# Node sums of a four-layer graph network by segmented running sums along the edges, stored to DRAM and gathered at each node's last edge, in place of one-hot products added into SBUF

## What is computed

```
x = ln(x + L0(x, edge_attr, src, dst))   # segment_sum(x[src] + edge_attr@We + b) -> MLP 64-128-64
x = ln(x + L1(x, src, dst))              # sum, sum of squares, max, min of x[src]; scalers by degree;
                                         # 768x64 product; batch norm; relu
x = ln(x + L2(x, src, dst))              # mean of x[src] @ w_l.T + x @ w_r.T + b
x = ln(x + L3(x, W, weight, src, dst, etype))  # segment_sum((x @ W[etype])[src] * weight)
```

## Time and profile before

| | |
|---|---|
| median of three runs | 16,712.28 us |
| the profiled execution, first to last instruction (span; the page gives no other time of it) | 22,127.4 us |
| POOL busy | 12,342.5 us (56%) |
| PE busy (matmul) | 8,912.5 us (40%) |
| DVE busy | 8,596.8 us (39%) |
| ACT busy | 1,783.1 us (8%) |
| mean traffic | 33 GB/s |

### The profile page before, as it was taken

The page is one execution under the profiler, slowest core; times in us unless marked ns, Lnnn a source line. Parts: engine busy times, 40 slices in busy tenths (PEclk is TensorE's granted clock), DMA queues, the critical chain, the costliest instruction groups (busy, mean ns, idle before and its releaser), DMA issues. The chain is left out here.

```text
span 22127.4 us, 244411 instructions
## 1 busy us (share of the span) xinstructions
PE 8912.5 (40%) x46268; PEld 7719.6 (35%) x46268; DVE 8596.8 (39%) x26793; ACT 1783.1 (8%) x5619; POOL 12342.5 (56%) x12921
## 2 busy tenths in 40 slices
PE   3444444445555555555553333333334333333333
PEld 3334333334544444444442222222223222222222
DVE  4333333333455555555553333333334333333333
ACT  0000000000222222222220000000001000000000
POOL 5555555555555555555545555655564555555555
PEclk6666666666677777777775555555555555555555
DMA  2222222221111111111111111111112111111111
GB/s 62 43 40 41 40 40 40 39 40 39 40 38 37 37 37 38 38 38 37 38 44 26 22 23 22 23 22 22 23 23 69 23 23 23 23 23 23 23 23 33
DMA packets 1780784, 739.62 MB, mean 33 GB/s; under 512 B 1449213, under 2 KB 1566897, under 8 KB 1777102
## 3 DMA queue, kind: packets, MB, share of 16 engines
q0 software_dynamic: 412800, 423.23, 10.0%
q1 hardware_dynamic: 1367936, 315.87, 7.1%
HBM read 669.74 MB, written 68.37 MB: 33 GB/s over the span
## 5 line engine op out<-in xcount | busy, mean ns | idle before, releaser
L1188 DVE TENSOR_TENSOR acc<-acc,ps_o 64x128 f32 (+2 forms) x12500 | 4373.1, 350 | 12651.9 <-remote 6628.2
L638 POOL DMA_INDIRECT work<-x_table,index x6250 | 5904.8, 945 | 4822.7 <-DMA window<-window_d 2837.1
L898 PE MATMUL ps_o<-work 128*64 128x128 f32 x12500 | 3079.6, 427 | 6978.2 <-issue 2381.0
L898 PEld LDWEIGHTS ps_o<-work 128*64 128x64 f32 x12500 | 2436.2, 223 | 7613.9 <-DVE acc L1188 4474.7
L638 POOL DMA_INDIRECT work<-x_in,index x3125 | 3001.3, 960 | 2400.2 <-DMA window<-window_d 1515.1
L638 POOL DMA_INDIRECT work<-xw_table,index x3125 | 2955.0, 946 | 2102.9 <-DMA window<-window_d 1106.8
L892 PE MATMUL ps_o<-work 128*66 128x128 f32 x6250 | 1692.7, 365 | 3127.2 <-DVE acc L1188 1371.0
L1164 DVE TENSOR_SCALAR work<-iota,meta 128x128 f32<-128x128 f32 x9375 | 2851.2, 304 | 69.8 <-issue 67.1
L895 PE MATMUL ps_o<-work 128*128 128x128 f32 x6250 | 1560.4, 339 | 2698.4 <-ACT work L707 1788.5
L892 PEld LDWEIGHTS ps_o<-work 128*66 128x66 f32 x6250 | 1083.7, 194 | 3308.3 <-DVE acc L1188 1887.2
L895 PEld LDWEIGHTS ps_o<-work 128*128 128x128 f32 x6250 | 1196.2, 238 | 2860.9 <-DVE acc L1188 1933.5
(11 more groups left out here) (201 smaller groups left out, 3977.0 us busy)
## 6 DMA issues: line engine op xcount, KB each, us to landing
work<-edge_attr SPq DMA_DIRECT2D x625, 160.0 KB
restart<-restart_d SPq DMA_DIRECT2D x625, 160.0 KB
work<-x_table,index POOLq DMA_INDIRECT x6250
work<-x_in,index POOLq DMA_INDIRECT x3125
work<-xw_table,index POOLq DMA_INDIRECT x3125
meta<-meta_d SPq DMA_DIRECT2D x2500, 7.5 KB
window<-window_d SPq DMA_DIRECT2D x2500, 0.0 KB
index<-src_e SPq DMA_DIRECT2D x1875, 2.5 KB
```

Source lines behind the costliest of these rows:

```text
L638: pool.indirect_dma_start(out=xs[:, q, k, col:col + D], out_offset=None, in_=table, in_offset=bass.IndirectOffsetOnAxis(ap=index[:, q, k:k ...
L898: ins = pe.matmul(sums[k][0:D, 0, :], xs[:, q, k, 0:D], s, start=True, stop=True)
L1188: dve.tensor_tensor(a, a, sums[k][0:n_rows, 0:halves, :], ALU.add).then_inc(L.added, 1)
```

## The change

The gathers of the edge phase stay as they are, 3,125 a layer in slots of five. Everything behind them is another method. PE turns the slot's rows so that features lie on partitions and 640 edges along the columns (`turn_in`). DVE runs one scan over the 640 columns (`scan`), whose factor is 0 at the first edge of a node and 1 elsewhere, so that the running sum starts anew with each node; it goes on from the last column of the slot before. In layer 1 there are two scans, one for sums and squares and one for maxima. PE turns the result back into rows (`turn_back`), ACT copies them from PSUM (`take_rows`) and stores all of them, for every edge, to a DRAM array `dump` (`dump_rows`), a DMA on ACT's own queue. A stored slot has 128 partitions of 2,560 bytes in layers 0 and 1 (two such stores in layer 1) and of 1,280 bytes in layers 2 and 3.

In the node phase POOL gathers, for each tile of 128 nodes, the row of each node's last edge from `dump`: 98 indirect DMAs a layer, 196 in layer 1 (two arrays). The row numbers come from a histogram of `dst` that PE and DVE make beside the first 62 turns of layer 0 (`one_hots`, `count_edges`: ten bf16 products a slot). A node phase has 14 groups of 7 tiles, written out without a loop. The dense products stay in f32; the bf16 parts are gone.

The core of the diff (`L.n` is the layer, `L.streams` 2 in layer 1 and 1 elsewhere):

```diff
-                def load_slot(turn, q, _, L=L):
-                    sp.wait_ge(L.added, block_no(turn, q, SUB))
-                    s = step_no(turn, q)
-                    rows = xw_rows_d if L.n == 3 else src_e
-                    sp.dma_start(index[:, q, :], rows[:, bass.ds(s * SUB, SUB)]).then_inc(meta_loaded[q], 16)
-                    sp.dma_start(meta[:, q, :], meta_v[:, bass.ds(s, 1), :].rearrange("p s f -> p (s f)")) \
-                        .then_inc(meta_loaded[q], 16)
-                    sp.dma_start(window[:, q, :], window_d.unsqueeze(0)[:, bass.ds(s * SUB, SUB)]) \
-                        .then_inc(meta_loaded[q], 16)
...
+                def load_slot(turn, q, L=L):
+                    if first(turn):
+                        return
+                    s = slot_no(turn, q)
                     if L.n == 3:
-                        sp.dma_start(weight[:, q, :], weight_e[:, bass.ds(s * SUB, SUB)]).then_inc(aux_loaded[q], 16)
+                        sp.wait_ge(L.prep, s + 1)
+                    else:
+                        sp.wait_ge(gathered[q], gathers_landed(L, turn - 1))
+                    sp.sem_inc(sp_past, 1)
+                    load_index(L, turn, q)
+                    for j in range(L.streams):
+                        sp.wait_ge(L.scan[j], s + 1)
+                    sp.sem_inc(sp_past, 1)
+                    load_flags(L, turn, q)
...
-                def scatter(turn, q, t, L=L):
-                    if t == 0:
-                        pool.wait_ge(L.rows_out if L.n else L.rows_set, step_no(turn, q) + (1, 3, 2, 2)[L.n])
-                        pool.sem_inc(pool_past, 1)
-                    pool.indirect_dma_start(
-                        out=agg[L.n], out_offset=bass.IndirectOffsetOnAxis(ap=node_of[:, q, t:t + 1], axis=0),
-                        in_=L.rows[:, q, t, 0:D], in_offset=None, bounds_check=N - 1, oob_is_err=False,
-                    ).then_inc(scattered[q], 16)
...
+                def gather(turn, q, L=L, table=table, col=col):
+                    pool.wait_ge(index_loaded[q], index_there(L, turn))
+                    for j in range(L.streams):
+                        pool.wait_ge(L.turned[j], slot_no(turn, q) + 1)
+                    pool.sem_inc(pool_past, 1)
+                    for k in range(SUB):
+                        pool.indirect_dma_start(
+                            out=xs[:, q, k, col:col + D], out_offset=None, in_=table,
+                            in_offset=bass.IndirectOffsetOnAxis(ap=index[:, q, k:k + 1], axis=0),
+                        ).then_inc(gathered[q], 16)
...
+                        for taken in (L.tp if L.n == 1 else [L.taken]):
+                            pool.wait_ge(taken, g - RING + 1)
+                    for t in range(GRP):
+                        for j in range(L.streams):
+                            pool.indirect_dma_start(
+                                out=L.agg[:, g % RING, t, j * L.span:(j + 1) * L.span], out_offset=None, in_=dump[L.n][j],
+                                in_offset=bass.IndirectOffsetOnAxis(ap=node_row[:, g * GRP + t:g * GRP + t + 1], axis=0),
+                            ).then_inc(agg_loaded[g % RING], 16)
...
+                        act.wait_ge(dumped[q], dumps_landed(L, turn - 1))
+                    elif L.n == 0:
+                        act.wait_ge(flags_stored, 32)
+                    for j in range(L.streams):
+                        act.wait_ge(L.back[j], SLOTS + s + 1)
+                        act.activation(L.rows[j][:, q], back_buffer(L, q, j)[:, 0:SUB * L.span], ACT.Copy) \
+                            .then_inc(L.rowed[j], 1)
...
+                def dump_rows(turn, q, L=L, dump_v=dump_v, chunk=chunk):
+                    s = slot_no(turn, q)
+                    for j in range(L.streams):
+                        act.wait_ge(L.rowed[j], SLOTS + s + 1)
+                        act.sem_inc(act_past, 1)
+                        act.dma_start(dump_v[j][:, bass.ds(s * chunk, chunk)], L.rows[j][:, q]).then_inc(dumped[q], 16)
...
-                    s = onehot[:, q, k, :]
-                    elif L.n == 1:
-                        pe.matmul(sums[k][:, 0, :], xs[:, q, k, D:3 * D], s, start=True, stop=True)
-                        ins = pe.matmul(sums[k][:, 1, :], turned[:, q, k, :], s, start=True, stop=True)
-                    else:
-                        ins = pe.matmul(sums[k][0:D, 0, :], xs[:, q, k, 0:D], s, start=True, stop=True)
-                    ins.then_inc(L.summed, 1)
...
+                def turn_back(turn, q, L=L):
+                    s = slot_no(turn, q)
+                    for j in range(L.streams):
+                        pe.wait_ge(L.scan[j], SLOTS + s + 1)
+                        pe.wait_ge(L.rowed[j], SLOTS + s if L.n < 2 or q == 0 else SLOTS - 1 + s)
+                        pe.sem_inc(pe_past, 1)
+                        to = back_buffer(L, q, j)
+                        for k in range(SUB):
+                            ins = pe.transpose(to[:, k * L.span:(k + 1) * L.span], scanned[j][0:L.span, q, k * P:(k + 1) * P],
+                                               ident[0:L.span, 0:L.span])
+                        ins.then_inc(L.back[j], 1)
...
-                def add(turn, q, k, L=L, n_rows=n_rows, halves=halves, first_rank=first_rank):
-                    if k == 0:
-                        _, first_rank["of"] = nc.values_load_multi_w_load_instructions(
-                            window[0:1, q, :], engines=[mybir.EngineType.DVE], min_val=0, max_val=N - 1,
-                            skip_runtime_bounds_check_because="a rank is less than the number of nodes")
-                    n = block_no(turn, q, k)
-                    dve.wait_ge(L.summed, CREDIT + n + 1)
-                    dve.wait_ge(L.added, CREDIT + n)
-                    a = acc[0:n_rows, 0:halves, bass.ds(first_rank["of"][k], P)]
-                    dve.tensor_tensor(a, a, sums[k][0:n_rows, 0:halves, :], ALU.add).then_inc(L.added, 1)
...
+                    for j in range(L.streams):
+                        dve.wait_ge(L.turned[j], SLOTS + s + 1)
+                        dve.wait_ge(L.back[j], s + 1)
+                        dve.wait_ge(L.scan[j], SLOTS + s)
+                        op0, op1 = (ALU.mult, ALU.add) if j == 0 else (ALU.add, ALU.max)
+                        dve.tensor_tensor_scan(scanned[j][0:L.span, q, :], flags[0:L.span, q, j, :],
+                                               turned_buffer(L, q, j)[0:L.span, 0:SE],
+                                               scanned[j][0:L.span, (q - 1) % SLOTS, SE - 1:SE], op0, op1) \
...
```

More of the change, by code:

```diff
@@ L56 @@
+LAST = N - (P - 1) * NT
+GRP = 7
+GROUPS = NT // GRP
+GW = GRP * D
+RING = 3
+assert GROUPS * GRP == NT and 0 < LAST < NT
+HB = 10
+HIST_TURNS = 62
+HIST_COLS = NT * D // 2
+HIST_LAST = BLOCKS - HIST_TURNS * SLOTS * HB
+NODE_TURN = 70
 AVG_D_LOG = 2.833
 EPS = 1e-5
-RESTART = -1e30
-F_REL, F_END, F_DST = 0, 5, 10
-FIELDS = 15
-XS_COLS = 192
-L0_ROWS = 66
-DEG, DST = 64, 65
-def pipeline(eng, turns, stages, parts=1, start=0):
-    for q in range(SLOTS):
-        for part in range(parts):
+RESTART = 2.0 ** 100
@@ L436, in flat @@
-        def flat(tiles):
-            return tiles.rearrange("p t f -> p (t f)")
+            L.streams, L.span = STREAMS[n], SPAN[n]
+            L.width = L.streams * L.span
+            chunk = SUB * L.span
+            L.rows = [rows_all[:, :, j * chunk:(j + 1) * chunk] for j in range(L.streams)]
+            L.turned = [ls(f"turned{j}") for j in range(L.streams)]
+            L.scan = [ls(f"scan{j}") for j in range(L.streams)]
+            L.back = [ls(f"back{j}") for j in range(L.streams)]
@@ L1449 @@
         "weight_e": turned(inputs["edge_weight"]),
+        "dst_e": turned(inputs["dst"]),
         "dst_n": arr("dst", EP, EW),
```

1722 lines of the change are left out of this document (767 added, 955 removed).

## The result

The changed kernel takes 17,282.72 us (median of four runs, 17,248.87 to 17,293.49) against 16,714.6 us for the kernel before (median of four, one more than in the table of the time before); the ratio is 1.0335 [1.0321, 1.035]. It is 3.4% slower where 0.4% faster was predicted, and lies above the range. The profiled execution took 17,273.66 us, so this time profile and timed runs agree.

A forecast was written before the change was run, and what follows sets the result against it. The prediction took POOL issuing 12,500 gathers back to back as the bound: 15,600 us, plus 20 for the head, 980 for node phases and 45 of rest, 16,645, given as 16,650 us; range 16,350 to 16,930.

The forecast's parts named there:

- All lie beside the gathers.: Edge phases: DVE, PE and ACT each need under 6.24 us a slot, so POOL's 15,600 us of gathers stays.
- 22 ns at most: Layer 0's gathers: the most the trace shows they could shorten when DVE's one-hots and their two-port mode go.
- The allowance of 10 us for DVE's pauses: Layer 0: row numbers after turn 62 and 6,272-column operations at turn 70 cost 10 us, inside the 45 kept.
- The head: Start of the kernel: POOL issues 25 gathers before PE's first turn, so it costs 20 us, not 52.8.
- The estimate of 51 us for the first turn of PE: Head: 27 us for flags, 5.6 for a store to land and 18 for constants come before PE's first turn.
- The node phases: Phases after each layer's edge phase: 165, 370, 300 and 145 us, 980 in sum against 1,014.4 before.
- The clock decides, to the slow side: Rival: PE gets 1.2 GHz in the node phases of layers 1 and 2, giving 16,780 us; chance 0.18.
- Its threshold: The clock rival decides above a node-phase sum of 1,093 us, 33 us over the median.
- The stores: Rival: stores lengthen gathers by 80 ns, 250 us in layer 1 alone: 16,900 us, or 17,650 in all layers; chance 0.12.
- the quick gathers: Rival: timed gathers are quicker than profiled ones and DVE set the time before: 12,850 us, halfway 14,750; chance 0.08.
- the lost interference: Rival: gathers shorten to 938 ns, 22 ns in layer 0 and 7 elsewhere, 134 us, giving 16,515; chance 0.08.
- the first paragraph's reading of the earlier trace: Profile before: POOL's 5,459.0 us of waits for `window` loads are mostly of the profile's making and left out.

The follow-up runs named there:

- c1: Changed kernel, layer-1 stores cut to 8 of 640 columns, layer 1's node phase gathering from layer 0's array, ACT's DMA issues kept: 17,266.54 us.
- c2: Changed kernel with one more ACT operation of 320 columns in each layer-1 slot, written to unused memory: 17,143.76 us.
- e2: Changed kernel with one more ACT operation per layer-1 slot, and ACT's copies and stores there one slot later: 16,925.34 us.
- b1: Changed kernel with ACT's layer-1 copies and stores one slot later, one-hots' iota in PSUM, PE's first credits before the constants: 16,757.58 us.
- c3: Changed kernel with two more DVE additions a slot, layer 2 with both operands in SBUF, layer 3 with one in PSUM: 17,550.95 us.
- c4: b1 with SyncE's constants loaded in parts behind turns 2 to 8, its wait for row numbers three turns later: 16,667.17 us.
- groups a and d: Two groups of edits of the changed kernel, run with slow SyncE instructions; the kernel before took 21,780 and 22,090 us beside them.
- group e: Group of edits of the changed kernel, run with quick SyncE instructions; the kernel before took 16,694 us beside them.
- d1: Changed kernel with two more ACT operations of 320 columns per layer-1 slot, run with slow SyncE instructions: 20,311.09 us.
- e1: Same kernel as d1, two more ACT operations per layer-1 slot of the changed kernel, with quick SyncE instructions: 17,501.79 us.
- d2: Same kernel as e2, one more ACT operation and later copies and stores in layer 1, with slow SyncE instructions: 20,110.16 us.

## Why the prediction was wrong

**The step that failed: "All lie beside the gathers."** It added up each engine's work in a slot (DVE 3.1, PE 2.2 to 4.3, ACT 3.0 us), found each under 6.24 us, and let POOL set the pace. The sums were right: the run after shows 1,541 us of DVE in 3,500, so 3.0 us a slot. But ACT and PE wait for each other in a closed ring, and there the times add: PE's 4.5 us at the granted 0.51, and ACT's preparing, last copy and two issues, come to 6.77 us. c1 (same ring, no stores) rules out the traffic; c2 against e2 (same work, same clock, ring whole and cut: 4,103 and 3,901 us) shows the ring. b1 got back 305 us of the 313, but with the clock at 0.69 beside the cut. The prediction had PE's 4.3 us at the low clock in its sum, and so found it harmless; in the ring the low clock costs time: c2's ring, with more work on ACT but at 0.69, is the shorter one. The order of the stages was in the code before the run; following one slot's chain through ACT's and PE's programs would have shown it.

**The same step in layer 0.** It left out that a DVE operation can hold POOL. The rule was looked at, but for the one-hots that go, with the two-port mode, and put at 22 ns at most; that the change brings two compares with both operands in SBUF (1.16 and 1.48 us a slot) was not asked. 1,550 gathers at 1,071 in place of 945 ns are 195 us; most of the rest of the 245 us are three gathers of 6.3 to 7.4 us beside the 6,272-column operations (17 us) and a wait of 28 us behind turn 62. The allowance of 10 us for DVE's pauses looked at PE, which waits for the scan. The 17 us are held gathers, and the 28 us came by a path that it did not have: SyncE stands 48 us for the row numbers that DVE makes, and POOL's `index` loads stand behind it. The Trainium skill states the rule behind the held gathers ("SBUF — State Buffer", Who interferes with whom): a VectorE instruction with two SBUF inputs contends with a GpSimd instruction that reads SBUF. These gathers read their row numbers in SBUF, and c3's layers 2 and 3 agree: 1,031 against 944 ns.

**The head, 61 us for 20.** The estimate of 51 us for the first turn of PE was not far off (PE gives its first credit at 61). But POOL did not get to issue 25 gathers before it: the credits themselves stand behind PE's wait for the constants. That alone is easily mended, and b1 shows that it brings nothing, since the index load of the sixth slot stands behind the constants on SyncE. c4 moved those as well, and the wait for the row numbers too, and its layer 0 ends 69 us before b1's.

**Right.** Layers 2 and 3 at 1.25 us a gather (3,908 and 3,906 us). The stores do not stretch the gathers: 945 ns in layer 1 at 170 GB/s, and e2 has 944 ns at 184 GB/s. DVE's scan at 1.54 us. The node phases of layers 0 and 3 to 10 and 1 us; of layer 1, 393 for 370. Layer 2's 325 for 300 is in part luck: it ran at a granted 0.50, for which the prediction's prices gave 386 us, and only the middle that it took between the two clocks came near.

**The rivals.** "The clock decides, to the slow side" named the node phases of layers 1 and 2, which came out 48 us over together; it missed that the clock also stretches a ring in the edge phase. Its threshold is off by 12 us as well: with 15,665 us for the other terms, "slower" (above 16,746) begins at a sum of 1,081 us, not 1,093. The stores, the quick gathers and the lost interference did not happen; the last went the other way. And the first paragraph's reading of the earlier trace rows had the wrong reason: POOL's 5,459 us of waits for `window` are not of the profile's making. They go with slow SyncE instructions, and with these the timed runs of groups a and d are 30 to 32% longer too. Leaving them out of the sum was right for the timed runs.

## What to carry to other kernels

Where two engines hand a slot to and fro, follow one slot through both programs and add up the closed chain; each engine's own sum below the pace proves nothing. A lag of one more slot on one side cuts such a chain; here the five buffers for it were there. Do the sum at the lower clock, for a chain through PE may fit under the pace at one clock and not at the other. Beside indirect gathers, give VectorE's large operations an operand in PSUM, or cut them short: both were worth more than 100 us here (layer 0's gathers fell from a mean of 1,071 ns to 946 and 993). And put an engine's first loads of the loop ahead of constants that are needed late.

## What the runs showed of the hardware

The TensorE clock in layer 1 is not a property of PE's work alone. PE was busy 2,298 of 3,500 us at a granted 0.51. With one short ACT operation added to each slot it was busy 2,082 us at 0.69, and the layer was shorter by 110 us: more work on ACT made it faster. That PE pauses longer in c2's slot is not shown to be the reason: with the ring cut and nothing added (b1) the slots are shorter and PE turns more blocks (11,192 in place of 10,332, busy 2,121 us), and the grant is 0.69 as well. What raises it was not found.

A gather that starts while a DVE operation with both operands in SBUF runs ends 0.82 us after that operation in the rows above, so a 6.67 us operation makes a gather of 7.41 us.

SyncE's plain register moves take 29 ns each at some times and 2 to 1,402 ns (median 29) at others, and its other instructions likewise. One and the same chip showed the slow moves in groups a and d and the quick ones in group e. On that chip the kernel before takes 32% longer with them (22,090 us in d, 16,694 in e) and variants of the changed one 16 to 19% (d1 against e1, d2 against e2), so the order of the two is turned round. What makes them slow was not found.
